# First stage of a graph and LSTM kernel: four root groups, other places for keys, negated products, constants and loads

## What is computed

```python
# x: 3125 nodes x 256; src, dst: 53125 edges sorted by dst in the inputs
h = layernorm(x) @ weight + bias
agg = segment_sum(h[src], dst, 3125)
x = x + agg / max(degree, 1)
# then an LSTM-like recurrence over layernorm(x), node after node:
#   i, o = sigmoid(...), g = tanh(...), each of x_t U + b + h V
#   c = h * c + i * g;  h = o * tanh(c)
x = x + h_of_every_node
```

## Time and profile before

| | us |
|---|---|
| median of three runs (480.34 to 482.78) | 481.91 |
| the profiled execution | 482.2 |
| its span | 480.4 |
| TensorE's products busy | 422.0 |
| VectorE busy | 358.7 |
| ScalarE busy | 345.3 |
| GpSimd busy | 186.3 |

### The profile page before, as it was taken

How to read it: one execution, slowest core, us unless ns; L and a number is a source line. 1 busy time by engine, 2 the same in 40 slices (tenths; PEclk the granted TensorE clock), 3 DMA queues, 4 the chain that set the end, 5 groups by cost and what they waited for, 6 DMA issues and landing times.

```text
span 480.4 us, 15515 instructions
## 1 busy us (share of the span) xinstructions
PE 422.0 (88%) x6106; PEld 368.8 (77%) x6106; DVE 358.7 (75%) x1139; ACT 345.3 (72%) x904; POOL 186.3 (39%) x322
## 2 busy tenths in 40 slices
PE   2876999979999999999999999986787779999992
PEld 2655887868897898888998888875677778888871
DVE  4897896987997878777786553346677778888884
ACT  1545997466876777777767655465899989999991
POOL 7721380356554546555454433221122222222220
PEclk9997899999999999999999999999999999999996
DMA  6642001330100001000100010001000000110111
GB/s 187 160 110 66 1 2 38 104 104 28 47 10 1 1 5 52 2 1 1 55 2 2 1 55 1 1 1 56 3 3 3 3 4 3 59 56 3 57 58 59
DMA packets 9604, 16.91 MB, mean 35 GB/s; under 512 B 2006, under 2 KB 7451, under 8 KB 9526
## 3 DMA queue, kind: packets, MB, share of 16 engines
q1 hardware_dynamic: 8076, 13.96, 9.3%
q0 software_dynamic: 880, 0.86, 0.9%
q10 hardware_dynamic: 570, 1.03, 0.8%
HBM read 6.23 MB, written 9.61 MB: 33 GB/s over the span
## 4 chain that ended last, share of the span: by engine, by line
PE 35%; DVE 32%; ACT 14%; issue 8%; POOL 7%; DMA 2%; SPq 0%; DVEq 0%; ACTq 0%; POOLq 0%
PE bank L1246 9%; PE bank L1212 8%; PE bank L1214 8%; ACT tc L1033 5%; DVE h L1815 5%; DVE h L1852 5%; DVE hots L1592 4%; DVE c_st L1810 4%; PE bank L1274 3%; PE bank L1165 3%; DVE h_flat L1815 3%; ACT counts L882 2%; POOL rstd L738 2%; POOL newton L737 2%; DMA gx<-in_dst_dram,gx 2%
## 5 line engine op out<-in xcount | busy, mean ns | idle before, releaser
L1165 PE MATMUL bank<-hots 128*128 128x125 f16 x625 | 120.8, 223 | 0.9 <-ACT counts L882 0.9
L1344 PE MATMUL bank<-h,V 128*128 128x62 f16 (+1 forms) x2952 | 103.1, 192 | 18.8 <-DVE h L1815 10.5
L1344 PEld LDWEIGHTS bank<-h,V 128*128 128x128 f16 x2952 | 94.9, 97 | 30.2 <-issue 27.8
L1592 DVE TENSOR_TENSOR hots<-iota,kp 128x1024 f16<-128x1024 f16 x160 | 108.6, 709 | 8.0 <-PE bank L1165 7.8
L1212 PE MATMUL bank<-h_flat,counts 125*128 125x257 f16 x375 | 97.2, 273 | 0.1
L1214 PE MATMUL bank<-h_flat,counts 125*128 125x256 f16 x375 | 96.3, 271 | 0.0
L771 POOL TENSOR_TENSOR hc<-h_flat,c_st 128x126 f32<-128x126 f32 x80 | 33.9, 424 | 97.1 <-DVE c_st L1810 92.2
L882 ACT ACTIVATE counts<-bank 125x500 f16<-125x500 f32 x96 | 55.9, 623 | 19.6 <-PE bank L1165 18.3
L1212 PE MATMUL bank<-h_flat,gx 125*128 125x257 f16 x250 | 68.2, 273 | 0.0
L1214 PE MATMUL bank<-h_flat,gx 125*128 125x256 f16 x250 | 67.4, 270 | 0.0
L1165 PEld LDWEIGHTS bank<-hots 128*128 128x128 f16 x625 | 57.5, 98 | 8.5 <-DVE hots L1592 1.2
(11 more groups left out here) (172 smaller groups left out, 804.4 us busy)
## 6 DMA issues: line engine op xcount, KB each, us to landing
h_dram<-h_flat SPq DMA_DIRECT2D x1, 3137.2 KB
x_dram<-x_sb SPq DMA_DIRECT2D x5, 625.0 KB
x_sb<-in_x_dram SPq DMA_DIRECT2D x4, 560.0 KB
out_dram<-x_sb SPq DMA_DIRECT2D x4, 560.0 KB
x_sb<-in_x_dram ACTq DMA_DIRECT2D x1, 560.0 KB
out_dram<-x_sb SPq DMA_DIRECT2D x1, 336.0 KB
x_sb<-in_x_dram SPq DMA_DIRECT2D x4, 65.0 KB
out_dram<-x_sb SPq DMA_DIRECT2D x4, 65.0 KB
```

The source lines that it names most:

```text
L1165: nc.tensor.matmul(ps_count[group % 3][:, pos * KEYS:(pos + 1) * KEYS], hots[:, ring, 0, g // 2, :, g % 2], hots[:, ring, 1, g // 2, 0:KEY ...
L1344: mm = nc.tensor.matmul(to[:, (m - m0) * n:(m - m0 + 1) * n], V16[:, v_part, d, m * P:(m + 1) * P], h16[:, h_part, d, c0:c1], start=False, ...
L1592: nc.vector.tensor_tensor(hots[:, k % RING, :, :, :, :].rearrange("p a h n g -> p (a h) n g"), iota[:, :, :].unsqueeze(1).to_broadcast(of) ...
```

## The change

The roots are taken in four groups instead of three (blocks 0 to 4, 5 to 9, 10 to 14, 15 to 24), in VectorE's blocks 5 to 7 and 12 to 13, and the statistics of blocks 15 to 24 are put in its blocks 9 to 12. Keys are placed in VectorE's blocks 4, 8 and 15 and turned in TensorE's blocks 6, 11 and 18. The negated product of block j - 3 stands behind the products of block j - 2. Blocks below 10 have one product that nobody reads. Part 1 of x is issued by SP, and parts 3 and 4 wait for the first edge gather. GpSimd fills only what is needed at once (`CONSTS` 4), does the next four fills and the negated identity once the row comparisons are done, and the pads of counts and line after the edge gathers; TensorE and SP wait for them (`later_set`).

```diff
@@ -67,9 +67,9 @@
     assert E == EDGE_ROWS * ROW_PARTS * ROW_LEN and BLOCKS % X_CHUNK == 0
 
 
-    NORMS = [(0, 5), (5, 10), (10, 25)]
+    NORMS = [(0, 5), (5, 10), (10, 15), (15, 25)]
     B_LOW = 32
-    CONSTS = 10
+    CONSTS, LATER = 4, 6
     assert OUTS * HOT_WINDOWS == P and BLOCKS == NORMS[-1][1]
 
     SIXTEENTHS = NB // 16 * 16
@@ -251,6 +251,7 @@
         col_set = sem("col_set")
         table_set = sem("table_set")
         z_pool = sem("z_pool")
+        later_set = sem("later_set")
         iotas = sem("iotas")
         consts = sem("consts")
         dve_seq = sem("dve_seq")
@@ -517,9 +518,9 @@
             return t + 1 - lows_dve(t)
 
 
-        TURN_KEYS = (5, 8, 10)
+        PLACE_KEYS, TURN_KEYS = (4, 8, 15), (6, 11, 18)
         HOTS_FROM, HOTS_LATER = 7, 3
-        WARM_FIRST, WARM_EACH = 14, 2
+        WARM_FIRST, WARM_EACH = 14, 1
         HOTS_AHEAD = 3
         FIRST_HOTS = OUTS + HOTS_AHEAD
 
@@ -581,9 +582,10 @@
                 for p0, p1 in SPLIT:
                     sp.dma_start(x_sb[p0:p1, js, :], x_steps[p0:p1, js, :]).then_inc(x_in[c], 16)
             load_x(0)
+            load_x(1)
             sp.wait_ge(rows_known, 1)
             load_x(2)
-            sp.wait_ge(win_rows_in[2], 16)
+            sp.wait_ge(win_edges_in[0], 16)
             for c in range(3, BLOCKS // X_CHUNK):
                 load_x(c)
             for in_ in win_edges_in:
@@ -594,6 +596,7 @@
                 with nc.allow_non_contiguous_dma("bias columns"):
                     sp.dma_start(gb[:, n, :], b.rearrange("(a p) -> p a", p=P)).then_inc(weights_in, 16)
 
+            sp.wait_ge(later_set, LATER)
             sp.wait_ge(line_low_act, lows_act(BLOCKS - 1))
             sp.wait_ge(line_low_dve, lows_dve(BLOCKS - 1))
             sp.dma_start(h_dram.rearrange("(j p) f -> p j f", p=NB), line).then_inc(line_stored, 16)
@@ -657,19 +660,20 @@
                                     pattern=[[-1, P]], channel_multiplier=1).then_inc(consts, 1)
             nc.gpsimd.iota(iota[:, :, :], pattern=[[1, P], [0, 2]], base=0, channel_multiplier=0,
                            allow_small_or_imprecise_dtypes=True).then_inc(consts, 1)
+            nc.gpsimd.memset(ones_row[:, :], 1.0).then_inc(consts, 1)
+            pool.wait_ge(consts, 4)
+
+
+            pool.wait_ge(before_ready, ROW_PARTS)
+            nc.gpsimd.memset(edges_p[96:P, :], -1.0).then_inc(later_set, 1)
+            pool.wait_ge(later_set, 1)
             nc.gpsimd.memset(ones16[:, :], 0.0).then_inc(ones_zero, 1)
             pool.wait_ge(ones_zero, 1)
-            nc.gpsimd.memset(ones16[0:1, :], 1.0).then_inc(consts, 1)
-            nc.gpsimd.memset(ones16[B_LOW:B_LOW + 1, :], 1.0).then_inc(consts, 1)
-            pool.wait_ge(consts, 5)
-            nc.gpsimd.memset(ones_row[:, :], 1.0).then_inc(consts, 1)
-            pool.wait_ge(consts, 2)
-            nc.gpsimd.tensor_scalar(minus_one[:, :], ident[0:NB, 0:NB], -1.0, None, ALU.mult).then_inc(consts, 1)
-            nc.gpsimd.memset(counts[0][:, :, :, NB:P], 0.0).then_inc(consts, 1)
-            nc.gpsimd.memset(line[:, :, 2 * D:LINE], 1.0).then_inc(consts, 1)
-            pool.wait_ge(consts, CONSTS - 1)
-            nc.gpsimd.memset(edges_p[96:P, :], -1.0).then_inc(consts, 1)
-            pool.wait_ge(consts, CONSTS)
+            nc.gpsimd.memset(ones16[0:1, :], 1.0).then_inc(later_set, 1)
+            nc.gpsimd.memset(ones16[B_LOW:B_LOW + 1, :], 1.0).then_inc(later_set, 1)
+            pool.wait_ge(later_set, 3)
+            nc.gpsimd.tensor_scalar(minus_one[:, :], ident[0:NB, 0:NB], -1.0, None, ALU.mult).then_inc(later_set, 1)
+            pool.wait_ge(later_set, 4)
 
             pool.wait_ge(rows_known, 1)
             for b in range(WIN_BATCHES):
@@ -684,6 +688,10 @@
                     win_edges[:, b, :, :].rearrange("p e a -> p (e a)"), None, dst_src,
                     bass.IndirectOffsetOnAxis(ap=start_i[:, b:b + 1].bitcast(U32), axis=0),
                 ).then_inc(win_edges_in[b], 16)
+            nc.gpsimd.memset(counts[0][:, :, :, NB:P], 0.0).then_inc(later_set, 1)
+            nc.gpsimd.memset(line[:, :, 2 * D:LINE], 1.0).then_inc(later_set, 1)
+            pool.wait_ge(later_set, LATER)
+
             weights_seq = [0]
 
             def halve(w, by):
@@ -832,10 +840,6 @@
                           w_gnn.rearrange("(a p) h -> p a h", p=P)).then_inc(w_in, 16)
             with nc.allow_non_contiguous_dma("bias to every partition"):
                 act.dma_start(w_sb[:, DH * D:(DH + 1) * D], b_gnn.partition_broadcast(P)).then_inc(w_in, 16)
-            x_steps = x.rearrange("(c t) d -> c t d", t=STEPS)
-            for p0, p1 in SPLIT:
-                act.dma_start(x_sb[p0:p1, X_CHUNK:2 * X_CHUNK, :], x_steps[p0:p1, X_CHUNK:2 * X_CHUNK, :]
-                              ).then_inc(x_in[1], 16)
 
             def deviation(n):
                 j0, j1 = NORMS[n]
@@ -896,8 +900,10 @@
             for j in range(BLOCKS + 3):
                 if j == 3:
                     deviation(1)
-                if j == 8:
+                if j == 7:
                     deviation(2)
+                if j == 13:
+                    deviation(3)
                 if j + 1 < BLOCKS and not z_by_pool(j + 1):
                     first_norm(j + 1)
                 if j < BLOCKS:
@@ -1181,15 +1187,11 @@
                 for k in first_counts(j):
                     for w in range(windows_of(k), windows_of(k + 1)):
                         count(w)
-                t = j - 3
-                if t >= 0 and not low_by_dve(t):
-                    pe.wait_ge(line_hi, t + 1)
-                    nc.tensor.matmul(bank[t % 2][0:NB, 0:D], minus_one[:, :], line[:, t, D:2 * D], start=False,
-                                     stop=True, skip_group_check=True).then_inc(line_left, 1)
                 t = j - 2
                 if 0 <= t < BLOCKS:
                     pe.wait_ge(zT_ready, t + 1)
                     if t == 0:
+                        pe.wait_ge(later_set, 4)
                         pe.wait_ge(w_split, 1)
                         pe.wait_ge(b_split, 1)
                     if t >= 2 and low_by_dve(t - 2):
@@ -1202,6 +1204,11 @@
                         mm = nc.tensor.matmul(bank[t % 2][0:NB, 0:D], zT[:, t % 3, z_part, d, :],
                                               W16[:, w_part, d, :], start=False, stop=(n == len(parts) - 1))
                     mm.then_inc(line_ps, 1)
+                t = j - 3
+                if t >= 0 and not low_by_dve(t):
+                    pe.wait_ge(line_hi, t + 1)
+                    nc.tensor.matmul(bank[t % 2][0:NB, 0:D], minus_one[:, :], line[:, t, D:2 * D], start=False,
+                                     stop=True, skip_group_check=True).then_inc(line_left, 1)
                 if j in TURN_KEYS:
                     turn_keys(TURN_KEYS.index(j))
                 if j < HOTS_FROM + HOTS_LATER:
@@ -1317,6 +1324,7 @@
                         if t == RUN:
                             pe.wait_ge(pads_set, 1)
                         if t == 0:
+                            pe.wait_ge(later_set, LATER)
                             pe.wait_ge(line_low_act, lows_act(BLOCKS - 1))
                             pe.wait_ge(line_low_dve, lows_dve(BLOCKS - 1))
                         if t >= 2:
@@ -1629,27 +1637,29 @@
                 if j >= 3 and low_by_dve(j - 3):
                     line_low(j - 3)
                 if j == 0:
-                    chunk_stats(7, 9)
+                    chunk_stats(7, 10)
                 if j == 1:
                     window_starts(1)
-                    chunk_stats(9, 10)
                     chunk_to_root(1)
                 if j == 2:
                     chunk_deviation(1)
                     window_starts(2)
                 if j == 3:
-                    chunk_stats(10, 12)
-                    edge_places(0)
-                if 4 <= j < 8:
-                    chunk_stats(3 * j, 3 * j + 3)
-                if j == 6:
-                    edge_places(1)
+                    chunk_stats(10, 13)
+                if j in PLACE_KEYS:
+                    edge_places(PLACE_KEYS.index(j))
+                if j == 5:
+                    chunk_stats(13, 15)
+                    chunk_to_root(2)
                 if j == 7:
+                    chunk_deviation(2)
+                if 9 <= j < 12:
+                    chunk_stats(15 + 3 * (j - 9), 18 + 3 * (j - 9))
+                if j == 12:
                     chunk_stats(24, 25)
-                    chunk_to_root(2)
-                if j == 8:
-                    chunk_deviation(2)
-                    edge_places(2)
+                    chunk_to_root(3)
+                if j == 13:
+                    chunk_deviation(3)
                 for k in first_hots(j):
                     one_hots(k)
             for k in range(OUTS, FIRST_HOTS):
```

## The result

The changed kernel takes 479.89 us (median of 20 runs) against 481.70 us, a ratio of 0.9972 with a 95% interval of 0.9958 to 0.9985: 0.7 to 2.0 us faster, 1.35 by the ratio. 3.5 us were forecast. A second series of the same pair gave 0.9968 (0.9941 to 0.9995).

What follows compares the result with a forecast made beforehand. VectorE paces the first stage to about 46 us, ScalarE from 54. Gains 2.9 (start) + 5.6 (waits), less 1.3 (root), 1.55 (new waits), 0.15 (GpSimd), give 5.5; less 1.75 (late keys), 3.75: 478.4 us, range 475.7 to 481.7.

Steps and rivals of the forecast that it cites:

- the start: Before block 0: VectorE starts its low half of z, T(0), at 15.4 us instead of 18.27, 2.9 us sooner.
- What bounds the kernel: First stage: VectorE sets the pace to about 46 us, ScalarE from about 54; what the stage saves, the kernel saves.
- With the same 1.0 us the first part is there at 8.5: Start: with the second part behind it on SP's queue, x's first part is ready for VectorE at 8.5, not 11.44.
- 5.6 (waits gone): VectorE, blocks 0 to 16: 1.52 us of waits for window rows and 4.1 for ScalarE's high half go.
- 1.55 (new waits): Turned keys: ScalarE's copies add waits of 1.05 us in block 6 and about 0.5 in block 11.
- The third rival: TensorE at 1.2 GHz in blocks 3 to 6 and most of 7 to 15; 4.65 us lost, 486.7 us; chance 0.07.
- 1.75 us behind T(16): Block 18: full ScalarE waits some 1.2 us for turned keys and copies for 0.55; bounds 0.6 and 3.0.
- Part 4: Early blocks: negated product behind the next products, taken as 0; bounds 0.1 us gained in four blocks, lost in eight.
- Part 1's comparisons: Row table at the start: without GpSimd's fills beside them, the fifth comparison ends at 7.2, 1.4 us sooner.
- part 2's wait: Window rows: with x's last parts held back, VectorE's 1.52 us wait for the fifth gather goes; bound 0.8 stays.
- The first rival: Clock falls to 1.2 GHz once in blocks 8 to 12, losing 2 to 2.9 us; 480.8 us, chance 0.22.
- if the clock falls there: Sign that the forecast is wrong: TensorE's clock falls between VectorE's low halves of blocks 7 and 16; no size given.

Runs made afterwards that it cites:

- e1: Changed kernel with part 1 of x issued by ScalarE's queue again, as before; ratio to the kernel before 1.0026 (1.0007 to 1.0044).
- e3: Changed kernel with SP waiting for weight and bias before it issues part 1 of x; ratio to the kernel before 0.9952 (0.9933 to 0.9970).
- e4: Changed kernel with the third turn of keys in block 25 instead of 18; ratio to the kernel before 0.9990 (0.9966 to 1.0014).
- g2: The kernel before once more, nothing edited, for a second trace; first sum at 78.70 us against 79.15, no ratio given.
- f4: The kernel before with one product that nobody reads in each early block instead of two; ratio to the kernel before 1.0012 (0.9988 to 1.0036).
- h3: The kernel before with only the negated product moved behind the next block's products; ratio to the kernel before 0.9987 (0.9963 to 1.0010).
- g1: The changed kernel once more, nothing edited, for a second trace; ratio to the kernel before 0.9968 (0.9941 to 0.9995).
- e2: Changed kernel with VectorE's row numbers ahead of the wait for weight and bias; ratio to the kernel before 0.9972 (0.9948 to 0.9996).
- h4: Changed kernel with the third turn of keys in block 16 instead of 18; ratio to the kernel before 0.9960 (0.9940 to 0.9980).
- f1: Changed kernel with two products that nobody reads in each block below 10 instead of one; ratio to the kernel before 0.9985 (0.9960 to 1.0010).
- g3: Changed kernel with part 1 of x held back, two unread products a block, third keys turned in block 16; ratio to the kernel before 0.9933, median 478.69 us.
- g4: Changed kernel with the negated product ahead of the next block's products again; ratio to the kernel before 0.9991 (0.9964 to 1.0019).
- f2: Changed kernel with part 1 of x held back for weight and bias and two unread products a block; ratio to the kernel before 0.9954 (0.9933 to 0.9976).

## Why the prediction was wrong

**The step that failed is the start.** The prediction's sum has 3.75 us at the first sums, and the profiled pair 1.51. It had T(0) 2.9 us sooner and measured 0.74, which is nearly all of the difference. The rest of the sum came out: T(0) to T(16) shrank by 2.43 us (2.6 forecast), and 1.66 were given back behind T(16) (1.75 forecast).

**What bounds the kernel**, VectorE before block 16, was right, and the waits for the root and the third keys left VectorE's path. T(0) to T(16) became 38.6 us in both traces of the changed kernel, where the sum gave 53.8 - 15.4 = 38.4. That closeness is in part luck: T(0) to T(7) was 12.5 where 11.7 were forecast, T(7) to T(16) 26.1 where 26.7 were, and with four cold blocks (e1, e3, e4) the whole is 40.8. The kernel before needs 41.0 in the trace that the prediction read and 39.7, 38.6 and 41.1 in g2, f4 and h3. The sign was right, the size not. By steps:

- "With the same 1.0 us the first part is there at 8.5": failed. It was waited for until 10.04 in the changed kernel's second trace and until 9.5 to 10.4 in six others with this order of loads. That second part and first share a queue does not make the first undisturbed; only with the second held back (e3) did the step come true, T(0) 15.41. In the first trace VectorE asked for x only at 10.70, because the bias, whose landing had no place in the sum, held the maximum until 9.50 and the row numbers until 10.37. T(0) was 0.7 and 1.4 us sooner in the two traces, not 2.9, counted from 18.27; the kernel before has 17.76 to 19.08 itself.
- "5.6 (waits gone)": right for the trace it was read from, too large as a base. The two waits together are 5.7, 4.5, 3.2 and 5.7 us in before, g2, f4 and h3. T(16) is 58.6 in the mean of these four (59.28, 58.81, 57.43, 58.85), not 59.28; the price of stalls that differ from trace to trace was taken from one. "1.55 (new waits)" was 1.72 in the first trace, all of it ahead of T(7); in e3 the early waits are 3.7.
- What an early start is worth: the sum let it pass to T(16) whole. In e3 a T(0) that was 2.1 us sooner gave T(7) = 30.12 for 30.00, with TensorE cold for four blocks instead of two. The third rival has the ring (2.7 us, as measured), but not the slowdown: the first blocks pay, and from T(7) to T(16) the clock did not matter. Its cause, half the filler, moves the count of cold blocks, but two fillers gave no time that can be told.
- "1.75 us behind T(16)": measured 1.3 with the clock up and 2.8 with it down, and another 0.3 between T(19) and the sums (14.5 against 14.2).
- Two small slips of its arithmetic: VectorE's blocks 7 to 15 are listed as 25.1 us, while the sum has 26.7 for T(7) to T(16) (26.1 measured, with no wait); and 478.4 is 3.75 less than the profiled 482.2, while 3.75 less than the median is 478.15.
- Part 4 at 0 was right, with 0.5 us in cold blocks. Part 1's comparisons (1.4 us) were 1.6, in the trace; part 2's wait went as forecast.
- The first rival named the clock's fall and nearly its place: in the changed kernel it is 0.78 from 44 to 48 us and 0.50 from 48 to 52, in VectorE's blocks 12 to 14. Its price, 2 to 2.9 us, was wrong: VectorE never waited, so the fall cost nothing. The prediction's own sign ("if the clock falls there") came true and was no cause.

The books of the two profiled traces: 0.74 at T(0), 2.43 more to T(16), less 1.33 at the keys, less 0.33 at the end are the 1.51 us at the sums; with 0.9 in the recurrence, and 0.3 between the first sum and the first state (263.5 us before, 263.2 in the changed kernel), they make 2.7, and the spans differ by 2.8. Neither the 0.9 nor the 0.3 was forecast. The medians differ by 1.8 and the ratio says 1.35. In the means over traces T(0) is 1.4 us sooner (17.1 in changed, g1, e2, e4 and h4 against 18.5) and T(16) 2.0 (56.6 against 58.6), so most of what reaches T(16) is the start. At the sums it is 1.1 us in the means of the changed kernel's two traces and 0.3 with e2 among them (78.13 against the old traces' 78.45). With the 1.2 behind the sums that is 1.5 to 2.3 us. The ratio's 1.35 (0.7 to 2.0) lies just below that; how often each state of the clock occurs in the timed runs was not seen.

One more fall of the clock lies between 325 and 340 us in e1, e3, e4, f1, f4, g3, g4, h3 and h4, not in the two traces of the changed kernel nor in the two of the kernel before:

```profile
325.00:340.00 15.00, 10.80 (x131) 0.78 0.12 44
```

(e1; us, TensorE busy, granted clock.) From the first sum to the first state on VectorE are then 264.6 to 265.4 us (e1: 346.3 - 81.67) and 263.1 to 263.6 without it (changed: 340.8 - 77.64, e2: 342.9 - 79.78), 1.5 us in the changed kernels. It falls in traces of old and new orders alike; why in some is open, and it is as large as the gain that is measured here.

## To carry to other kernels

A stall can have a different length in every execution (2.2 to 4.2 us here): read its price from several traces before it goes into a sum. An early start is worth only what the bound behind it lets through: look there before it is counted in full. A load that is not wanted yet can delay the one in front of it on the same queue. Try the parts of a change alone and together: here neither large part gave anything alone, and one of them brings a wait that only the other removes.

## What was not expected of the hardware

A load queued behind another on the same queue still delayed the other's landing, here from 8.6 to about 10 us, and a little more from another queue. The bias, 128 KB and issued near 1.2 us, landed 6.1 or 8.3 us later in two traces of the same kernel; the weight ahead of it, 256 KB, took 3.8 and 4.0. TensorE, busy without a break from 15.98 us on with products at the 1.2 GHz length, reached 2.4 GHz only in the group that began at 24.89 in e3, and between 18 and 20 us in f1 and f2. In the changed kernel it had reached it by 16.7 and lost it again by 19. The granted clock of the windows read 1.00 in e3 all the while.
